# Products with the relative values: two runs of 64 matmul instructions for every four steps instead of eight pieces of 16

## What is computed

```python
q, k, v = proj(Wq, bq), proj(Wk, bk), proj(Wv, bv)        # 16 heads of 16 features, from layernorm(x)
idx = clip(key - query, -64, 64) + 64
rk, rv = embK[idx], embV[idx]                             # a key and a value vector per distance
w = softmax(q @ k.T + einsum('bhqd,qkd->bhqk', q, rk))
out = w @ v + einsum('bhqk,qkd->bhqd', w, rv)             # the second term: the relative values
x = x + layernorm(out @ Wo.T + bo)
x = x + layernorm(layernorm(x) @ ternary(Wf).T + bf)
```

## Time and profile before

| | |
|---|---|
| median of 3 runs | 2661.18 us (2657.5 to 2662.87) |
| the profiled execution | 2678.59 us, of which the span of instructions is 2676.8 us |
| granted TensorE clock, mean over the span | 0.938 |
| busy: PE, DVE, ACT, POOL | 95%, 76%, 58%, 36% |

### The profile page before, as it was taken

How to read it: one execution, slowest core, us unless ns; L and a number is a source line. 1 busy time by engine, 2 the same in 40 slices (tenths; PEclk the granted TensorE clock), 3 DMA queues, 4 the chain that set the end, 5 groups by cost and what they waited for, 6 DMA issues and landing times.

```text
span 2676.8 us, 100468 instructions
## 1 busy us (share of the span) xinstructions
PE 2534.3 (95%) x42130; PEld 1959.7 (73%) x42130; DVE 2022.9 (76%) x5187; ACT 1553.2 (58%) x2993; POOL 969.2 (36%) x2275
## 2 busy tenths in 40 slices
PE   5899999999999999999999999999999999999994
PEld 4477777777777777777777777777777777777773
DVE  4777678876887778876788767887688777887774
ACT  2456665556565655565655566556666556666651
POOL 3114323433345333453244432444333533341026
PEclk8699999999999999999999999999999999999997
DMA  7656654556445564555645656456644556445410
GB/s 225 180 143 183 172 157 131 142 170 193 144 135 164 153 181 138 159 162 159 172 136 145 185 161 168 129 142 181 178 147 147 137 168 188 141 144 157 134 34 25
DMA packets 605039, 408.96 MB, mean 153 GB/s; under 512 B 149162, under 2 KB 604330, under 8 KB 604330
## 3 DMA queue, kind: packets, MB, share of 16 engines
q1 hardware_dynamic: 604586, 402.54, 52.6%
HBM read 206.84 MB, written 194.90 MB: 150 GB/s over the span
## 4 chain that ended last, share of the span: by engine, by line
PE 73%; DVE 16%; issue 4%; ACT 2%; POOL 2%; DMA 1%; SPq 0%; DVEq 0%; POOLq 0%; ACTq 0%
PE oacc L793 16%; PE logitsT L755 15%; PE scores L733 14%; PE logitsT L760 7%; DVE maxes L1012 6%; DVE junk L1009 6%; PE misc L856 4%; PE misc L690 4%; PE misc L806 3%; PE misc L818 2%; PE misc L707 2%; PE misc L830 2%; ACT wxr L1212 1%; PE misc L843 1%; DVE stats L915 1%
## 5 line engine op out<-in xcount | busy, mean ns | idle before, releaser
L1009 DVE CUSTOM_DVE_ANT_1 junk<-scores,bands 128x512 bf16<-128x512 f32 x988 | 679.4, 688 | 427.9 <-PE scores L733 408.9
L755 PE MATMUL logitsT<-qs,ks 98*128 98x128 bf16 (+1 forms) x8192 | 980.6, 221 | 20.0 <-ACT wxr L1212 13.2
L1212 ACT ACTIVATE wxr<-logitsT 128x512 f32<-128x512 f32 x1024 | 586.0, 605 | 419.4 <-PE logitsT L755 379.3
L1212 ACT ACTIVATE wy<-logitsT 128x512 f32<-128x512 f32 x1024 | 591.0, 598 | 402.3 <-PE logitsT L755 389.3
L755 PEld LDWEIGHTS logitsT<-qs,ks 98*128 98x128 bf16 (+1 forms) x8192 | 664.2, 99 | 212.2 <-issue 76.2
L733 PE MATMUL scores<-ks,qs 96*128 96x256 bf16 (+6 forms) x3712 | 681.7, 289 | 54.8 <-DVE maxes L1012 31.6
L1012 DVE TENSOR_REDUCE maxes<-scores 128x1 f32<-128x512 f32 x1024 | 702.3, 686 | 1.9 <-PE scores L733 1.9
L760 PE MATMUL logitsT<-ident,bands 128*128 128x128 f32 x2048 | 463.7, 278 | 0.0
L733 PEld LDWEIGHTS scores<-ks,qs 96*128 96x128 bf16 (+1 forms) x3712 | 287.8, 98 | 207.5 <-DVE maxes L1012 112.3
L1240 POOL TENSOR_SCALAR rs<-rs 128x1 int32<-128x1 int32 (+1 forms) x224 | 45.8, 204 | 822.5 <-DVE rs L920 811.9
L760 PEld LDWEIGHTS logitsT<-ident,bands 128*128 128x128 f32 x2048 | 292.4, 143 | 43.4
(11 more groups left out here) (136 smaller groups left out, 2638.3 us busy)
## 6 DMA issues: line engine op xcount, KB each, us to landing
bs<-praw SPq DMA_DIRECT2D x256, 512.0 KB, 3.7
bands<-bs SPq DMA_DIRECT2D x224, 512.0 KB, 4.8
ks<-kd SPq DMA_DIRECT2D x64, 384.0 KB, 4.5
qs<-qd SPq DMA_DIRECT2D x112, 192.0 KB
bands<-bs SPq DMA_DIRECT2D x128, 128.0 KB, 3.9
qd<-qparts SPq DMA_DIRECT2D x64, 192.0 KB, 3.0
kd<-kparts SPq DMA_DIRECT2D x64, 192.0 KB, 2.6
qd<-qparts SPq DMA_DIRECT2D x64, 128.0 KB, 2.4
```

The costliest lines, as they stand in the source:

```text
L755: mm = e.matmul(lt[:, c * P:(c + 1) * P], kk[0:depth, h, kt * P:(kt + 1) * P], qs[i][0:depth, h, :], start=True, stop=not near, skip_group ...
L1009: e.tensor_tensor_reduce(junk[:], scores[:, 0:512].rearrange("p (a c) -> p a c", a=2), banded, 1.0, LOWEST, ALU.add, ALU.max, mx[:, h, 0:1 ...
L1212: e.activation(dst, src, ACT.Exp).then_inc(exp_ready, 1)
```

## The change

The four pieces of a part become one stage at slot 30 (31.5 for part 1) of the quad, that is 64 profile instructions in a row. Its bank is then given like any other stage's, and DVE's masking takes the slot of the stage.

```diff
         if i == QUAD - 1:
             for part in range(2):
-                for piece in range(4):
-                    at(z + 29.7 + 1.5 * part + 0.35 * piece, "relative", quad, part, piece)
+                at(z + 30 + 1.5 * part, "relative", quad, part)
...
-            bank = held if stage == "relative" and k[2] else until.index(min(until))
-            if stage == "relative" and k[2]:
-                slot += kept
-            else:
-                late, slot = max(0, until[bank] - slot), max(slot, until[bank])
-            if stage == "relative":
-                held, kept = bank, late if k[2] == 0 else kept
-            until[bank] = slot + (10 if stage == "relative" and k[2] < 3 else HOLD[stage])
+            bank = until.index(min(until))
+            slot = max(slot, until[bank])
+            until[bank] = slot + HOLD[stage]
...
-                    quad, part, piece = k
+                    quad, part = k
                     pe.wait_ge(merged, 2 * QUAD * (quad + 1))
                     pe.wait_ge(*free)
                     pe.wait_ge(reltab_ready, 8)
-                    for i in range(8 * part + 2 * piece, 8 * part + 2 * piece + 2):
+                    for i in range(8 * part, 8 * part + 8):
...
-                    if piece == 3:
-                        mm.then_inc(rel_summed, 1)
+                    mm.then_inc(rel_summed, 1)
...
-                elif stage == "relative" and k[2] == 3:
-                    quad, part, _ = k
+                elif stage == "relative":
+                    quad, part = k
                     dve.wait_ge(rel_summed, 2 * quad + part + 1)
```

More of the change, by code:

```diff
@@ L186, in with_banks @@
     timed, until = [], [-1000.0 - i for i in range(NMISC)]
-    held = kept = 0
     for slot, stage, k in sorted(slots, key=lambda x: x[0]):
@@ L263, in counts @@
             for stage, k in orders[engine]:
-                if stage in stages and not (stage == "relative" and k[2] < 3):
+                if stage in stages:
                     n += 1
@@ L281, in misc_banks @@
             continue
[L282 to L288, removed]
+        plan[(stage,) + k] = (bank,) + free[bank]
+        signal = FREED_BY[stage]
+        free[bank] = (signal, 1 if stage == "ternary" else value[(signal, stage) + k])
     return plan
```

## The result

The changed kernel took 2669.18 us (median of 7 runs, 2667.81 to 2671.44) against 2661.18 us before (7 runs, 2656.88 to 2663.78): ratio 1.0035, 95% interval 1.0025 to 1.0045, 8 us slower. The forecast was 2677.4 us in a range of 2666 to 2686, slower with 0.85. Sign and mechanism were right; the loss is half of what I had worked out.

A forecast was written before the change was run, and what follows sets the result against it. PE sets the pace and DVE follows, both full in the changed stretch. 14 tail quads x 1.02 + 3 bare x 0.95 - 14 projection x 0.07 = +16.2 us on 2661.2 gives 2677.4 us, range 2666 to 2686.

The forecast's parts named there:

- head e's scores get their second bank at 1051.83: Tail quad 11: the fifth head's scores wait for DVE's late maximum of the fourth; loss 1.02 us.
- The prices: PE's runs: 0.13 us plus 0.0184 us per instruction, so 1.30 us for 64; entering a run 0.09 us more.
- rival C: A run of 64 takes 1.60 us, not 1.30: 19 us more, 2696 us; chance 0.04.
- projection quads: 14 quads where the key projection stands between two heads' scores: gain 0.07 us each.
- A run's price of 0.22 us: PE: each run that disappears saves 0.13 + 0.09 us.
- The hand-over: From a run's end on PE to DVE's masking: 0.19 us; 0.14 or 0.25 would move the sum under 2 us.
- tail and bare quads: 14 quads with output work lose 1.02 us each; 3 with nothing between second and third heads' scores lose 0.95.
- The projection: PE's key projection between second and third heads' scores: 1.90 us, covering the wait for DVE there.
- The last quad: Two runs before and after, PE waiting for other chains: nothing, within 0.5 us.
- The basis: Whole kernel: the sum of +16.2 us put on the runs' median, 2661.2 us, not the profiled 2678.6.
- Rival A: PE's own work decides: tail quads gain 0.97 us, projection 0.61, bare 1.06; 25 us, 2636 us; chance 0.06.
- Rival B: The delay is made up later in PE's idle time: 2661 to 2666 us; chance 0.10.

The follow-up runs named there:

- before_again: The kernel before, unedited, profiled a second time: 2659.19 us, ratio 0.9997.
- the repeat: The changed kernel once more, timed against the kernel before: 2667.70 us, ratio 1.0034.
- proj_behind: Against the kernel before, runs of 64 only in key-projection quads and the last, DVE's masking order as before: 2652.09 us, ratio 0.9965.
- pairs: Against the kernel before, pieces of 32 instructions instead of 16, DVE's order as before: 2655.52 us, ratio 0.9980.
- last_only: Against the kernel before, runs of 64 and the change's early masking in quad 31 alone: 2659.73 us, ratio 0.9992.
- proj_only: Against the kernel before, the change in the 14 quads with key projection only: 2656.68 us, ratio 0.9982.
- tail_only: Against the kernel before, the change in the 14 quads with output work only: 2672.68 us, ratio 1.0046.
- mask_behind: The changed kernel with DVE's old order, both maskings lagging 0.75 slots: 2655.43 us, ratio 0.9981 to the kernel before.
- mask1_behind: The changed kernel with only part 1's masking lagging 0.75 slots: 2651.53 us, ratio 0.9963 to the kernel before.
- best: proj_behind plus pieces of 32 in the other quads and the change's runs and early masking in the last: 2646.18 us, ratio 0.9958 to before.

## Why the prediction was right, and where it was off

*DVE's order is the cause.* Shown: the same PE program with DVE's old order is 12 to 14 us faster. The step "head e's scores get their second bank at 1051.83" is seen in the profile after, with the two idle gaps of PE as told; PE's idle time ahead of scores rose from 57.2 us to 84.6, within the 20 to 30 forecast. The row of before_again, to be read beside that of line 722 above:

```profile
L733 PE MATMUL scores<-ks,qs 96*128 96x256 bf16 (+6 forms) x3712 | 677.8, 288 | 57.2 <-DVE maxes L1012 31.6
```

*The prices.* Run of 64: 1.30 us forecast, 1.30 measured in quad 11; all but two of the changed kernel's 64 runs lie within 0.04 us of 1.30, and rival C is out for them. One exception is the last run of the kernel; the other is the first run of quad 9, 2.26 us to the next group. PE, changed kernel, quad 9:

```profile
880.98 1.33 PE L795 MATMUL misc<-wxr,reltab 128*32 128x64 f32 x59
883.00 0.32 PE L795 MATMUL misc<-wxr,reltab 128*32 128x64 f32 x5 [0.69 <-issue]
883.25 0.61 PE L722 MATMUL scores<-ks,qs 96*128 96x256 bf16 x4
883.70 1.94 PE L679 MATMUL misc<-xnT,wk 128*128 128x256 f32 x8
885.48 0.61 PE L722 MATMUL scores<-ks,qs 96*128 96x256 bf16 x4
```

This is not chance alone: of the seven profiles with a run of 64 in this place six have it longer (1.69 to 2.26 us; 1.99 in the repeat), `proj_behind` has 1.31, and the five profiles with pieces there have nothing of the kind. So quad 9 alone is 0.79 us longer than before, where the other projection quads are 0.2 shorter; why is open. A run's price of 0.22 us stands behind the replay of `pairs`, right to 0.02 us.

*The hand-over* was one mis-sized term. I took 0.19 us from a run to the masking, from ACT's row; DVE starts 0.13 and 0.14 us after it in quad 11, and 0.15 us at the median of the 62 places. In tail and bare quads the chain to e passes through both maskings, and with 0.01 to 0.02 us less in some steps of DVE's maximum each stretch ended some 0.1 us earlier: tail 0.94 for 1.02, bare 0.84 for 0.95. I had said that 0.14 us would move the sum by less than 2 us; by my own replay it is 0.05 us twice in 17 quads and once in 14, 2.4 us.

*The projection* was the other. In projection quads the chain passes through one masking only, so the hand-over explains a third of their -0.22 for -0.07 at most. The projection between b and c took 1.90 us to the next group in the rows, 1.83 in before_again, but 1.73 or 1.78 behind a run of 64 (883.70 to 885.48 above); why it is shorter there is not shown.

Together the stretches of quads 0 to 30 give 13.1 + 2.1 - 2.0 = 13.2 against 16.2. The bare ones include quad 29 at 0.37 only, where the kernel before had a chance gap, and the projection ones quad 9.

*The last quad* I had put at nothing within 0.5 us. It gave back 1.2 to 1.6 us, and the part behind its sum 1.3 to 2.5 us more (spans 10.2 and 8.6 us apart, 12.7 and 9.8 at the last sum). What of it is the change and what is chance is open: last_only gave 1.3 us with an interval that holds zero, and an untouched last quad was 1.09 us shorter in proj_only. From the start of the last stretch to the end it is 57.9 to 60.2 us in the four profiles whose last quad is that of before and 55.5 to 58.2 in the other eight; before_again, from which I count, is the longest of all twelve, 1.1 us above the mean of its four. So part of the 2.5 to 4.1 us is the base. The timed medians are divided as well: set against the sum of their stretches of quads 0 to 30, tail_only, proj_only and pairs are 0.5 to 0.9 us faster than it, the change, its repeat, mask_behind and mask1_behind 2.8 to 5.2, but last_only, proj_behind and best only 0.7 to 1.4.

*The basis.* The sum was added to the median, which was right, though the rows came from an execution at a lower clock; as PE's stretch times differ little (10.39 us against 10.34 in quad 11), that hardly bent the replay, except for the projection (1.90 us against 1.83). Rival A fell in tail and bare quads; in projection quads the truth lies between it and my forecast, and `mask_behind` reaches most of it there (0.52 of 0.61). Rival B fell.

So the forecast of 16.2 us stands against 8.0 measured (9.3 in the repeat). By the profiles, 10.2 and 8.6 us apart from before_again, it is 13.2 and 12.8 in the stretches, less 4.1 and 2.5 at the end; the remainder, +1.1 and -1.8, are single differences elsewhere. About 3 us of the miss, net, thus lie in the replay of the stretches, and most of the rest lies at the end, where I can't tell the change from chance. The shift of 0.37 us in five projection quads is not the change's. It is this wait of PE for a DVE maximum, far behind the stretch, in quad 1:

```profile
305.52 0.39 PE L722 MATMUL scores<-ks,qs 96*128 96x512 bf16 x1 [0.21 <-DVE maxes L1000]
```

The repeat, with the same two programs, has it in none of the quads, while pairs and proj_behind have it in all five. PE and DVE meet there within a hair, and a small difference between executions or kernels decides whether PE waits.

## What to carry to other kernels

Where two engines hand work to and fro and both are full, merging pieces of a filler is two changes: one of the filler engine's overhead, and one of where the consumer's step stands in its queue. Price them apart, and keep the consumer's step behind the work that the producer waits for next, unless the consumer would stand idle there anyway (part 0's masking in `mask1_behind`). The same merge gained where something else stood between the dependent steps and lost where it didn't, so it should be chosen place by place; a replay of one stretch per kind was good to 0.1 us, and to 0.15 in projection quads; hand-over times should come from rows of the same pair of engines.

## What was unexpected of the hardware

- One execution of a single-core kernel showed a granted clock of 0.95 in its windows from 200 to 2000 us (1.00 in the two others whose windows were read; the span's mean was 0.938 there and 0.981 to 0.986 in the other eleven profiles), and was 17 us longer than its kernel's median. A profile's own clock must be read before its times are compared with another's.
- PE stands still for some tenths of a microsecond up to 1.5 us at single places, put down to nothing that the profile shows ("issue"), and the places come again from execution to execution: between 237 and 241 us of the span in all twelve profiles (0.27 to 0.56 us), between 712 and 720 us in four of them (1.0 to 1.5 us), in the first run of quad 9 in five of the seven that have a run of 64 there (0.33 to 0.69 us). A single profile shows only some of them; two profiles compared place by place need a repeat.
